# Fewer signals from TensorE in a graph layer: one per two products, with the transpositions and most sums left unsignalled

## The reference, cut to what matters

```python
w_m = (efeat @ W_msg + b_msg).reshape(E, in_f, -1)
w_a = (efeat @ W_attn + b_attn).reshape(E, in_f, -1)
h_src = feat[src][:, :, None]
e1, e2 = w_m * h_src, w_a * h_src
ex = jnp.exp(e2 - seg_max[dst])
denom = segment_sum(ex, dst)
ft = segment_sum(e1 * ex / denom[dst], dst).sum(axis=1)
```

## Time and profile before

| | us |
|---|---|
| median of 3 runs | 3181.63 (3181.13 to 3204.2) |
| the profiled execution | 3216.98 |
| its span, first to last instruction | 3215.1 |
| TensorE busy | 2134.1 (66%) |
| VectorE busy | 1858.7 (58%) |
| GpSimd busy | 1686.0 (52%) |
| ScalarE busy | 1255.2 (39%) |

### The profile page before, as it was taken

The page is one execution under the profiler, slowest core; times in us unless marked ns, Lnnn a source line. Parts: engine busy times, 40 slices in busy tenths (PEclk is TensorE's granted clock), DMA queues, the critical chain, the costliest instruction groups (busy, mean ns, idle before and its releaser), DMA issues. The chain is left out here.

```text
span 3215.1 us, 21756 instructions
## 1 busy us (share of the span) xinstructions
PE 2134.1 (66%) x6682; PEld 953.8 (30%) x6682; DVE 1858.7 (58%) x2902; ACT 1255.2 (39%) x1228; POOL 1686.0 (52%) x1845
## 2 busy tenths in 40 slices
PE   2336678667787566766565558687777786667487
PEld 1212233223333222322222223233333332223233
DVE  6235466556665545655454456465667665666386
ACT  3113344334443334433333335353435444343354
POOL 6666555555564554444454444556565664536614
PEclk8657888878898787888887779888899998878799
DMA  6100000000000000000000000000000001001000
GB/s 210 15 14 10 11 10 10 10 9 9 9 14 9 9 9 8 8 12 8 8 9 7 8 7 12 9 9 11 8 12 11 9 12 22 11 7 16 8 1 3
DMA packets 60073, 47.60 MB, mean 15 GB/s; under 512 B 28366, under 2 KB 55439, under 8 KB 59436
## 3 DMA queue, kind: packets, MB, share of 16 engines
q0 software_dynamic: 57632, 29.73, 7.2%
q1 hardware_dynamic: 2316, 16.38, 1.4%
HBM read 44.00 MB, written 1.90 MB: 14 GB/s over the span
## 5 line engine op out<-in xcount | busy, mean ns | idle before, releaser
L652 POOL DMA_INDIRECT AR<-in_xt,AR x1607 | 1538.7, 958 | 751.3 <-issue 494.1
L1128 PE MATMUL PX<-AR,CS 128*128 128x512 f32 x3246 | 1660.3, 640 | 13.5 <-ACT AR L894 8.5
L1472 DVE CUSTOM_DVE_ANT_1 AR<-PW,AR 128x1024 f32<-128x1024 f32 x815 | 978.6, 1221 | 1172.2 <-remote 924.1
L1108 PE MATMUL PW<-WS,LT 100*128 100x512 bf16 x1630 | 551.7, 425 | 976.2 <-DVE AR L1472 755.0
L1128 PEld LDWEIGHTS PX<-AR,CS 128*128 128x128 f32 x3246 | 668.9, 207 | 633.6 <-issue 516.3
L888 ACT ACTIVATE LT<-PTB 100x1024 bf16<-100x1024 bf16 (+1 forms) x221 | 211.3, 956 | 1437.3 <-remote 1017.1
L1485 DVE TENSOR_TENSOR AR<-AR,PX 128x1024 f32<-128x1024 f32 (+1 forms) x442 | 501.2, 1134 | 113.8 <-ACT PX L944 87.1
L1108 PEld LDWEIGHTS PW<-WS,LT 100*128 100x128 bf16 x1630 | 140.0, 102 | 1398.0 <-DVE AR L1472 811.6
L946 ACT ACTIVATE AR<-AR 128x2048 f32<-128x2048 f32 (+1 forms) x221 | 413.0, 1869 | 7.2
L950 ACT ACTIVATE PX<-AR 128x1024 f32<-128x1024 f32 (+1 forms) x221 | 212.3, 961 | 330.7 <-DVE AR L1485 263.0
L657 POOL DMA_INDIRECT AR<-in_es,E0I x48 | 45.4, 946 | 556.2 <-issue 271.9
(11 more groups left out here) (192 smaller groups left out, 517.8 us busy)
## 6 DMA issues: line engine op xcount, KB each, us to landing
AR<-in_xt,AR POOLq DMA_INDIRECT x1607
AR<-in_eat SPq DMA_DIRECT2D x3, 3128.0 KB
AR<-in_eat SPq DMA_DIRECT2D x1, 3120.0 KB
y_d<-AR SPq DMA_DIRECT2D x1, 784.0 KB
AR<-y_d SPq DMA_DIRECT2D x1, 784.0 KB
AR<-in_es,E0I POOLq DMA_INDIRECT x48
y_d<-AR POOLq DMA_INDIRECT x36
CS<-in_cst SPq DMA_DIRECT2D x1, 442.0 KB, 5.3
```

The costliest lines, as they stand in the source:

```text
L652: g.indirect_dma_start(feat(h, j - j0, j - j0 + 1), None, xt, bass.IndirectOffsetOnAxis(ap=node, axis=0)).then_inc(hg_sem(h), 16)
L1108: i = pe.matmul(PAIRS[s % 2][:, j, :], LT[:, g % 3, lo:lo + 128], WS[:, :], start=True, stop=True)
L1128: i = pe.matmul(PDR, IDN, x, start=(a == 0 and j == 0), stop=(g == LAST[k] and j == n - 1))
L1472: v.tensor_tensor_reduce(em(g, j, j + 2).rearrange("p (x c) -> p x c", c=32), w, hb, 1.0, LOW, ALU.mult, ALU.max, accum_out=MXC[:, k % 2, ...
```

## The change

The copy of a transposed group and the preparation of the buffers of chunk k no longer wait for `p_T` but for a number of `p_W` that implies it: the products of a later pair, which TensorE makes after the transpositions. To make that number come soon, the transpositions move ahead of the last pair of products of the step (`T(p + 2)` now stands in the round before the last pair of p, at its head). `p_T` stays for the first two groups.

Of the products only every second pair signals: pairs 1 and 3 of a group of eight slots, 1 and 2 of a group of six. That is 442 signals of `p_W` in place of 815. Pair 0 is swept only when pair 1 is done too, and pair 2 of eight slots when pair 3 is.

Of the sums 72 groups still signal `p_g`: the last of each chunk (49), and those whose buffer is wanted so soon that the product's number would come too late (`LATE`, of which 25 groups, two of them also last). The others are waited for through a number of `p_W`. In all 516 signals.

No matmul, sweep or transfer is added or taken away.

```diff
+PAIRED = [x % 2 == 1 or 2 * x + 2 == GRP[g][2] for g in range(NGR) for x in range(GRP[g][2] // 2)]
+READY = [sum(PAIRED[:next(t for t in range(s, len(PAIRED)) if PAIRED[t]) + 1]) for s in range(len(PAIRED))]
+TURNED = [READY[1]] * 2
+for g in range(2, NGR):
+    x = GRP[g - 2][2] // 2 - 1
+    TURNED.append(READY[FROM[g - 2] + x])
+SUMMED = []
+for g in range(NGR):
+    later = [q for i, (q, _) in enumerate(STEPS) if q is not None and i >= USED[g] + 2]
+    SUMMED.append(READY[FROM[later[0]] + GRP[later[0]][2] // 2 - 1] if later else 10 ** 6)
+LATE = {OLD[g] for g in range(NGR) if OLD[g] is not None and SUMMED[OLD[g]] > READY[FROM[g]]}
+TOLD = sorted(set(LAST) | LATE)
...
                 def evac(g):
                     n = GRP[g][2]
-                    a.wait_ge(S["p_T"], g + 1)
+                    if g < 2:
+                        a.wait_ge(S["p_T"], g + 1)
+                    else:
+                        a.wait_ge(S["p_W"], TURNED[g])
                     if g >= 3:
-                        a.wait_ge(S["p_W"], FROM[g - 2])
+                        a.wait_ge(S["p_W"], READY[FROM[g - 2] - 1])
...
-                    i.then_inc(S["p_T"], 1)
+                    if g < 2:
+                        i.then_inc(S["p_T"], 1)
...
-                    i.then_inc(S["p_W"], 1)
+                    if PAIRED[s]:
+                        i.then_inc(S["p_W"], 1)
...
-                        if j == n - 1:
+                        if j == n - 1 and g in TOLD:
                             i.then_inc(S["p_g"], 1)
...
                     for x in range(4):
+                        if p is not None and p + 2 < NGR and x == GRP[p][2] // 2 - 3:
+                            T(p + 2)
                         if x < len(ahead):
                             W(*ahead[x])
                         if old is not None:
                             gsum(old, 2 * x, 2 * x + 2)
-                        if x == 1 and p is not None and p + 2 < NGR:
-                            T(p + 2)
...
                     if j == 0:
                         v.wait_ge(S["v_hm"], HMS[g])
                         if OLD[g] is not None:
-                            v.wait_ge(S["p_g"], OLD[g] + 1)
-                    v.wait_ge(S["p_W"], s + 1)
+                            if OLD[g] in TOLD:
+                                v.wait_ge(S["p_g"], TOLD.index(OLD[g]) + 1)
+                            else:
+                                v.wait_ge(S["p_W"], SUMMED[OLD[g]])
+                    v.wait_ge(S["p_W"], READY[s])
```

More of the change, by code:

```diff
@@ L141 @@
 HMS = [x + 1 for x, seg in enumerate(SEGS) for g in seg]
+PAIRED = [x % 2 == 1 or 2 * x + 2 == GRP[g][2] for g in range(NGR) for x in range(GRP[g][2] // 2)]
+READY = [sum(PAIRED[:next(t for t in range(s, len(PAIRED)) if PAIRED[t]) + 1]) for s in range(len(PAIRED))]
+INDEX = {q: i for i, (q, _) in enumerate(STEPS) if q is not None}
+TURNED = [READY[1]] * 2
[8 more added lines that the diff above has]
+TOLD = sorted(set(LAST) | LATE)
 FINS = {USED[LAST[k]]: k for k in range(NC)}
@@ L884, in evac @@
                     n = GRP[g][2]
-                    a.wait_ge(S["p_T"], g + 1)
+                    if g < 2:
+                        a.wait_ge(S["p_T"], g + 1)
+                    else:
+                        a.wait_ge(S["p_W"], TURNED[g])
                     if g >= 3:
-                        a.wait_ge(S["p_W"], FROM[g - 2])
+                        a.wait_ge(S["p_W"], READY[FROM[g - 2] - 1])
                     a.activation(LT[:, g % 3, 0:128 * n], PTB[0:K, 0:128 * n], ACT.Copy).then_inc(S["a_T"], 1)
                 def sums(k):
-                    a.wait_ge(S["p_g"], LAST[k] + 1)
+                    a.wait_ge(S["p_g"], TOLD.index(LAST[k]) + 1)
                     if k >= 1:
@@ L910, in first @@
                     if k >= 2:
-                        a.wait_ge(S["p_T"], LAST[k - 2] + 1)
+                        a.wait_ge(S["p_W"], TURNED[LAST[k - 2]])
                     a.activation(part(k, 99, 100)[:, 1:d, :], VLD[:, 1:d].unsqueeze(2), ACT.Relu, bias=1.0, scale=-1.0).then_inc(S["a_p"], 1)
@@ L1445, in low @@
                     if k >= 2:
-                        v.wait_ge(S["p_T"], LAST[k - 2] + 1)
+                        v.wait_ge(S["p_W"], TURNED[LAST[k - 2]])
                     x = RM[:, 0:DEG[k], :]
```

## The result

The changed kernel takes 3373.65 us (3360.81 to 3387.35) where the kernel before, run beside it, takes 3183.88 (3181.13 to 3204.2). The ratio is 1.0582 [1.0517, 1.0647]: it is 5.8% slower. The profiled execution took 3360.81 us.

A forecast was written before the change was run, and what follows sets the result against it. While gathers stream, TensorE's signals were taken to wait in a line, coming out one by one. Gains of 167 and 45 minus losses of 76 and 30 made 106 us less: 3077 us, 3.3% faster, range 2850 to 3240.

The forecast's parts named there:

- What bounds the kernel: Whole run: while gathers stream, TensorE's signals are held and come out one by one; stopped gathers let compute catch up.
- Fewer signals in held time: Beyond 10 us of each gather burst: 5.9 us a pair in place of 8.3, 54 more pairs, 167 us gained.
- The clock: TensorE at the start of bursts: less idling in held time raises its clock, 45 us gained (0 to 89).
- Pairing outside held time: Gaps and first 10 us of bursts: later sweeps and once-per-chunk VectorE work stop TensorE, 76 us lost (0 to 150).
- Longer bursts: GpSimd's gather bursts: shorter gaps join bursts, six joins in 90, 30 us lost (0 to 60).
- Transpositions: TensorE's moved transpositions and waits through later products: nothing, with 0 to 40 us more if the copy is late.
- The count of pairs: Sweep busy time divided by 1.30 us: 296 pairs at burst starts, 134 beyond 10 us, 272 in gaps.
- One sign: VectorE's waits outside bursts: the forecast fails if they exceed 200 us.
- The gate opens for all: Rival, 8%: held signals come out together when a gate opens, so their number doesn't matter; only costs stay, 3287 us.
- Pairing starves both: Rival, 12%: in quiet time, lock-step of sweep, signal and products costs TensorE 1.0 us per signal; slower, 3280 us.
- A signal is cheap: Rival, 8%: held news has another origin, each signal costs 0.03 us, 22 us in all; 3160 us.
- A lone signal is served sooner: Rival, 10%: in a line of one, a signal's price may be half, 2.7 us; 2698 us.

The follow-up runs named there:

- doubled_2: Kernel before plus a second, unread signal on the first of each two products (2072 signals), with signals held: 3229.24 us, 1.0011 times the kernel before.
- no_pairs_again: Changed kernel without pairing: every product pair signals, transpositions moved and unsignalled, 72 sums signal; signals held: 3254.2 us, 1.0195 times the kernel before.
- after_third: The changed kernel unaltered, run once more with signals held: 3356.44 us, 1.0527 times the kernel before.
- pairs_moved: Changed kernel, but transpositions keep their own waited-for signals and all sums signal (884 signals); signals held: 3369.64 us, 1.0557 times the kernel before.
- filled_2: Changed kernel with every dropped signal put back on a semaphore nobody reads (1257 signals), signals held: 3367.38 us, 1.0446 times the kernel before.
- doubled: Kernel before plus a second, unread signal on the first of each two products (2072 signals), no signals held: 2242.79 us, 1.0001 times the kernel before.
- landed: Kernel before with some 170 short breaks in GpSimd's gathers, waiting until earlier ones landed; no signals held: 2481.45 us, 1.1075 times the kernel before.
- sums_only: Kernel before with only the sums' signals thinned to 72 of 221 (1108 signals), no signals held: 2252.34 us, 1.0002 times the kernel before.

## Why the prediction was wrong

**What bounds the kernel: right in part.** In the held condition signals of TensorE do come late while gathers run, and what isn't done in bursts is done in gaps; the sum of bursts (1992 to 1999 us in each held trace) and the gaps account for the time. But I took it for a property of the kernel. Free runs with an unbroken stream show no held signal, so the stream alone doesn't make it.

**"Fewer signals in held time": the step that failed.** It gave each signal a price D of 5.4 to 7.8 us, as if a line served one in so many us whatever stood in it. Removing signals then had to be worth 167 us. In the runs, pairs beyond 10 us take (the last column has all pairs done in bursts, of 757 or 758, in 1992 to 1999 us each time):

| | signals | of products waited for | us for a pair | pairs in bursts |
|---|---|---|---|---|
| before | 1257 | each | 8.1 | 459 |
| `doubled_2` | 2072 | each | 8.2 | 458 |
| `no_pairs_again` | 889 | each | 8.1 | 441 |
| after, `after_third` | 516 | every second pair | 9.5, 9.4 | 418, 410 |
| `pairs_moved` | 884 | every second pair | 9.3 | 415 |
| `filled_2` | 1257 | every second pair | 10.1 | 417 |

The rate follows the third column and not the second. A rate of one signal in 5.4 us (5.3 with the pairs counted) is right as an average of before, but it isn't the price of a signal: those that nobody waits for ride along. What a held signal costs falls on the wait for it. Before, two buffers' signals could be on their way, one sweep's work behind each; with pairing one signal is on its way and both buffers wait for it. That pairing costs this is shown; that it is the lone signal which costs, and not the later start of the first sweep of two, is argued from the order of the code and the stretch above, for no run parts them. I had this round in the sum ("only one signal of products can now be on its way"), at D + 3.2 + 0.16 D, but at a D that the fewer signals were to keep at 5.4 to 7.8 us. It came out at 10.8 us for a wait, and a round of 1.84 pairs took 1.84 x 9.5 = 17.5 us instead of 9.5 to 12.2. Even with D = 10.8 the sum gives 15.7 us, so D is the larger part of the error and not all of it. The direction of that lengthening is shown. That a wait has to do with the burst's end goes with the 54 of 84 waits that end there; but a burst also ends because VectorE stands and buffers fill, so it isn't shown which brings the other.

The Trainium skill ("TensorE: Matmul & The Clock Gate", The cost: per-tile semaphore tail) has about 26.3 ns for each increment, fitted where small matmuls packed into one array all signal. Carried over to `doubled`'s 815 more, that would be, an estimate, 21 us. The runs here don't agree with carrying it over: 2242.79 beside 2243.36, at most 2.2 us.

**The clock: it did not come.** 45 us were to come from less idling of TensorE in held time. It idles more there (40% busy, 48% before), the mean clock is 0.822 and busy time 2125.7 where 2134.1 was: 8 us. The term hung on the first one.

**Pairing outside held time: too dear.** I took 76 us off. Gaps went from 2.83 to 2.88 us a pair, 339 x 0.05 = 17 us; the first 10 us of bursts from 2.75 to 2.83, 296 x 0.08 = 24, in part held already. From 1492.78 us on, ten pairs take 22.9 us in a quiet stretch, within the 22 to 25 forecast. Free, pairing alone costs 7 to 9 us. The whole change costs 31 us there though its parts cost 7 and 5; why they do more together isn't settled.

**Longer bursts: right in sign, and larger than thought without pairing.** The changed kernel has 85 bursts for 90. `no_pairs_again` has 77, and its 1.95% lie here: for a pair it is as quick as before in every kind of time, but 1243 us lie beyond 10 us of a burst and not 1107. So its bursts hold 441 pairs and not 459; 18 x 2.8 = 50 us is the estimate, 61 us were measured. So this step, at 30 us, was under-sized.

**Transpositions: not nothing.** I costed their move and the waits through products at zero. Free, together, they cost 0.16%. Held, either they or the waits through later products (of copies, buffers or sums) make the 1.95%, by way of longer bursts: `pairs_moved`, with the move but own signals, equals the changed kernel, so with pairing on, the waits through products add nothing (1.0557 and 1.0527). Alone in the held condition the two were not measured. Nor is it settled what TensorE's waits for the copy cost: 336.3 us in the changed kernel, 191.1 in `pairs_moved`, which is as slow, 40.1 in `no_pairs_again`.

**The count of pairs.** 296, 134 and 272 should have been 323, 136 and 298 (the divisor 1.30, above). Held time hardly changes by it; a pair moved out of the gaps is worth 2.8 us and not 3.1, so the 167 us would have been about 150. It isn't what failed. One sign was badly chosen too: VectorE's sweep waits 319 us outside bursts now, but it waited 217 there before, so 200 us could tell nothing.

**The rivals.** "The gate opens for all" came nearest, 3287 us where 3374 came: held waits got longer as signals got fewer (10.8 us; its sign said 15), and the number of signals doesn't matter. But `filled_2` waits 11.2 us each (1001.1 us, 89 times) with all signals back, so it is not the fewer signals that lengthen them. The rival missed what pairing costs in the gate. I argued against it with two sweeps 15.56 us apart; `doubled_2` shows that such a spacing isn't a price per signal. "Pairing starves both" (3280 us) had the right cause, pairing, in the wrong place: the quiet time. "A signal is cheap" was right on the signal (nothing in either condition) and wrong that nothing else was at stake. "A lone signal is served sooner" is refuted: 7.8 us became 10.8.

**Left open.** What sets the held condition; whether thinning the stream ends it (`landed` met only free conditions, where it loses 10 to 11%); pairing without the moved transpositions, held; which of the lone signal and the later sweep costs; and the mechanism by which a signal comes after 8 us once and 24 us the next time. No version beat the kernel before: `doubled` and `sums_only` equal it, all others are slower wherever they ran.

## What to carry to other kernels

A signal that nobody waits for cost nothing measurable here, so counting signals was no way to find time; ask for each wait how many signals that could end it are on their way at once. Pairs with two on their way took 8.1 to 8.2 us where delivery was late, those with one 9.3 to 10.1. An average rate in a trace (one signal in 5.4 us) is a price only once a run has added or removed the thing alone: `doubled` is a two-line edit, and where signals were held it settled the main term. And run the kernel before beside every variant, since here the same kernel took 2242 and 3193 us on the same chip 430 s apart.

## What was unexpected in the hardware

On some occasions completed work of TensorE is seen by VectorE and ScalarE 10 to 33 us late while GpSimd's gathers stream (the stretches of rows 3 and at 1456 to 1493 us), and 3184 to 3227 us come of 2242 to 2253, 42% more; on others, with the same stream of 1607 gathers at 1.25 us, never. Within a sitting the condition didn't change between kernels; between two sittings on one chip, 430 s apart, it did. VectorE's news to TensorE was not late in the same burst: the read-out at 1483.53 ended at 1483.61 and products started at 1483.67. And 815 more increments of a semaphore cost nothing that a measurement can tell, in either condition (1.0001 and 1.0011).
